# Sixth layer of a fused six-layer block: the norm of the next tile, the rounding of its x and the products of its scales move from VectorE to GpSimd

## Chip, cores and metric

One core of a Trainium2 chip runs the whole program in one launch. The metric is device time in microseconds (us); the median of 3 runs of the kernel before is 2464.33 us (2462.03 to 2466.09). DVE is VectorE, ACT is ScalarE, PE is TensorE, POOL is GpSimd, SP is SyncE.

## The reference, cut to the sixth layer

Six layers follow one another on x of 64x32 tokens by 256 channels: three attention or FFN layers with a cross attention first, then again cross attention, attention, and a mixture of experts. The change touches the last one alone:

```
x = x + _L1_ffn_ref(_layernorm(x), router_w, gate_w, up_w, down_w)

xq     = clip(round(x * s), -128, 127) / s,   s = 127 / max(max|x|, 1e-5)    # per token
combine = top-2 of softmax(x @ router_w.T), renormalised to sum 1
for e in range(8):
    gate, up  = xq @ gate_q[e].T, xq @ up_q[e].T          # 256 -> 512, ternary weights
    activated = up * square(relu(gate))
    y_e       = quant(activated) @ down_q[e].T            # 512 -> 256
    out      += combine[:, e] * y_e
```

The input of the layer is normalised per token (mean and variance over 256 channels), and the experts see it rounded to whole numbers; the scales of input and weights are multiplied back later.

## The kernel before, in words

The 2048 tokens are 16 tiles of 128 tokens, one per partition. x stays in SBUF (`x_all`) through all layers. Each layer is a phase with one hand-written instruction stream per engine; semaphores alone order the engines against one another, and every instruction that needs the result of the one before it on its own engine waits for it too (`link`).

In the sixth phase (`experts`) the weights of all 8 experts are in SBUF already, as bf16. A tile is worked as 4 pairs of experts, u = 0 to 3. For a pair, PE multiplies the rounded input with the gate and up weights of two experts into four PSUM banks (L2592), ACT takes relu and square (L2409, L2413), DVE multiplies by the up half (`products`, L2504), takes the largest magnitude of each token and computes the scales on 2 columns (`sizes`, L2520 to L2528). ACT adds the magic number that rounds (L2420), DVE subtracts it and clamps to bf16 (`clamp`, L2514), PE turns the tile (L2604), ACT copies it (L2430), PE multiplies by the down weights (L2616), and DVE adds the scaled result to x (`output`, L2538). Clamp runs one pair later and output two pairs later, so the pipeline runs on across tiles.

The next tile's input is prepared inside the current tile's steps. After pair 0 of tile t, DVE runs `rounded(t+1)`: norm to `f_xn` (L154), largest magnitude (L2460), scale and its reciprocal (L2461, L2462), x times scale plus magic number to `f_nxf` (L2463), minus magic number and clamp to bf16 `f_nx` (L2464), then square and cube of the scale and the product with the 8 weight scales to `f_kf` (L2465 to L2467). PE turns `f_xn` in pair 1 for the router and `f_nx` in pair 2 (L2568, L2579). DVE runs the router's softmax parts after pairs 2 and 3. `f_kf` is read by L2523 and L2526 of the following tile. `rounded(0)` stands before the loop. GpSimd does nothing in this phase but one memset at its start (L2379).

Of the kernel before, what the change touches and what calls it, by code (L numbers as in the profile page):

```python
# [18 lines left out]
ALU = mybir.AluOpType  # L19
# [3 lines left out]
P = 128  # L23
# [4 lines left out]
NT = B * S // P  # L28
# [5 lines left out]
MAGIC = 12582912.0  # L34
# [5 lines left out]
NE, IE = 8, 512  # L40
# [44 lines left out]
def build(nc, d, out):  # L85
# [2227 lines left out]
    def experts(sb):  # L2313
# [27 lines left out]
        xn_ready, xT_psum, xT_ready = shared("xn_ready", 1, NT), shared("xT_psum", 1, NT), shared("xT_ready", 1, NT)  # L2341
        lg_psum, lg_in, lg_exp = signal("f_lg_psum"), signal("f_lg_in"), signal("f_lg_exp")
        nx_ready, nxT_psum, nxT_ready = signal("f_nx_ready"), shared("nxT_psum", 1, NT), shared("nxT_ready", 1, NT)
        link = chain("f_link", 20)
        PAIRS = NE // 2
        up_psum, rg_done, sq_done, a_done = (signal("f_up_psum", NE), signal("f_rg_done", NE), signal("f_sq_done", NE),
                                             signal("f_a_done", NE))
# [29 lines left out]

        def pool(eng):
            eng.memset(magic[:, :], MAGIC).then_inc(magic_ready.sem, 1)  # L2379

# [62 lines left out]
        def vector(dve):  # L2445
            norm_vector(dve, n)
            dve.wait_ge(wr_loaded.sem, wr_loaded.at(1, 0))
            wlink_n = chain("f_wlink2", 3)
            w3 = f_ws[:, 0, :].rearrange("p (e k) -> p e k", k=3)
            wlink_n.link(dve, dve.tensor_tensor(ec[:, 0, :], w3[:, :, 0], w3[:, :, 0], ALU.mult))  # L2450
            wlink_n.link(dve, dve.tensor_tensor(ec[:, 0, :], ec[:, 0, :], w3[:, :, 1], ALU.mult))
            wlink_n.link(dve, dve.tensor_scalar(ec[:, 1, :], w3[:, :, 2], 1.0 / 127.0, None, ALU.mult))
            wlink_n.end()

            def rounded(t, s):
                link.at(t)
                normed(dve, xn[:, :], t).then_inc(xn_ready.sem, 1)
                dve.wait_ge(xn_ready.sem, xn_ready.at(t, 1))

                link.link(dve, dve.tensor_reduce(xs[:, 0:1], xn[:, :], AX.X, ALU.max, apply_absolute_value=True))  # L2460
                link.link(dve, dve.tensor_scalar(xs[:, 0:1], xs[:, 0:1], EPS, 1.0 / 127.0, ALU.max, ALU.mult))  # L2461
                link.link(dve, dve.reciprocal(xs[:, 1:2], xs[:, 0:1]))  # L2462
                link.link(dve, dve.tensor_scalar(nxf[:, :], xn[:, :], xs[:, 1:2], MAGIC, ALU.mult, ALU.add))  # L2463
                dve.tensor_scalar(nx[:, :], nxf[:, :], MAGIC, 127.0, ALU.subtract, ALU.min).then_inc(nx_ready.sem, 1)  # L2464
                link.link(dve, dve.tensor_tensor(xs[:, 2:3], xs[:, 0:1], xs[:, 0:1], ALU.mult))  # L2465
                link.link(dve, dve.tensor_tensor(xs[:, 3:4], xs[:, 2:3], xs[:, 0:1], ALU.mult))
                link.link(dve, dve.tensor_scalar(kf[s][:, :], ec[:, 0, :], xs[:, 3:4], None, ALU.mult))  # L2467

            def router_scores(t, s):

                dve.wait_ge(lg_psum.sem, lg_psum.at(t, 1))
                link.link(dve, dve.tensor_copy(lg[:, 0, :], ps[:, 1, 0:NE]))
                link.link(dve, dve.tensor_reduce(ls[:, 0:1], lg[:, 0, :], AX.X, ALU.max))
                dve.tensor_scalar(lg[:, 1, :], lg[:, 0, :], ls[:, 0:1], None, ALU.subtract).then_inc(lg_in.sem, 1)

            def router_shares(t, s):
                dve.wait_ge(lg_exp.sem, lg_exp.at(t, 1))
                link.link(dve, dve.reciprocal(ls[:, 2:3], ls[:, 1:2]))
                link.link(dve, dve.tensor_scalar(lg[:, 3, :], lg[:, 2, :], ls[:, 2:3], None, ALU.mult))

                pj, pi = spread(lg[:, 3, :], 1, NE), spread(lg[:, 3, :], 2, NE)
                dve.tensor_tensor(cmp_[:, 0, :, :], pj, pi, ALU.is_gt)
                link.link(dve, dve.tensor_tensor(cmp_[:, 1, :, :], pj, pi, ALU.is_equal))
                link.link(dve, dve.tensor_tensor(cmp_[:, 1, :, :], cmp_[:, 1, :, :], lower[:, :, :], ALU.mult))
                link.link(dve, dve.tensor_tensor(cmp_[:, 0, :, :], cmp_[:, 0, :, :], cmp_[:, 1, :, :], ALU.add))
                link.link(dve, dve.tensor_reduce(lg[:, 4, :], cmp_[:, 0, :, :], AX.X, ALU.add))
                link.link(dve, dve.scalar_tensor_tensor(lg[:, 5, :], lg[:, 4, :], TOP_K - 0.5, lg[:, 3, :],
                                                        ALU.is_lt, ALU.mult))
                link.link(dve, dve.tensor_reduce(ls[:, 3:4], lg[:, 5, :], AX.X, ALU.add))
                link.link(dve, dve.reciprocal(ls[:, 4:5], ls[:, 3:4]))  # L2490
                link.link(dve, dve.tensor_scalar(cmb[s][:, :], lg[:, 5, :], ls[:, 4:5], None, ALU.mult))
                link.link(dve, dve.tensor_tensor(oc[s][:, :], cmb[s][:, :], ec[:, 1, :], ALU.mult))
                link.end()

            def step(t, s, more, first=False):
                elink.at(t)

                def products(u):
                    for k in range(2):
                        e = 2 * u + k  # L2500
                        dve.wait_ge(sq_done.sem, sq_done.at(t, e + 1))
                        if k == 0 and not (first and u < 2):
                            dve.wait_ge(nh_done.sem, nh_done.at(t, u - 1))
                        dve.tensor_tensor(act_[u % 2][:, k, :], ps[:, 3 + 2 * k, :], rg2[k][:, :], ALU.mult)\  # L2504
                            .then_inc(a_done.sem, 1)

                def clamp(u):

                    if u >= PAIRS or (first and u < 0):
                        return  # L2510
                    dve.wait_ge(q_done.sem, q_done.at(t, u + 1))
                    if not (first and u < 2):
                        dve.wait_ge(hT_psum.sem, hT_psum.at(t, u - 1))
                    dve.tensor_scalar(nh[u % 2][:, :, :], act_[u % 2][:, :, :], MAGIC, 127.0, ALU.subtract, ALU.min)\  # L2514
                        .then_inc(nh_done.sem, 1)

                def sizes(u):
                    am, two = ams[u], slice(2 * u, 2 * u + 2)
                    dve.wait_ge(a_done.sem, a_done.at(t, 2 * u + 2))
                    dve.tensor_reduce(am[:, 0, :], act_[u % 2][:, :, :], AX.X, ALU.max, apply_absolute_value=True)\  # L2520
                        .then_inc(max_done.sem, 1)
                    dve.wait_ge(max_done.sem, max_done.at(t, u + 1))
                    elink.link(dve, dve.tensor_tensor(am[:, 1, :], am[:, 0, :], kf[s][:, two], ALU.mult))  # L2523
                    elink.link(dve, dve.tensor_scalar(am[:, 1, :], am[:, 1, :], EPS, None, ALU.max))
                    elink.link(dve, dve.reciprocal(am[:, 2, :], am[:, 1, :]))
                    dve.scalar_tensor_tensor(am[:, 3, :], am[:, 2, :], 127.0, kf[s][:, two], ALU.mult, ALU.mult)\  # L2526
                        .then_inc(size_done.sem, 1)
                    dve.tensor_tensor(am[:, 4, :], am[:, 1, :], oc[s][:, two], ALU.mult)  # L2528

                def output(u):  # L2530

                    if first and u < 0:
                        return
                    dve.wait_ge(y_psum.sem, y_psum.at(t, u + 1))
                    x = x_all[:, t if u >= 0 else t - 1, :]
                    for k in range(2):
                        dve.wait_ge(y_out.sem, y_out.at(t, 2 * u + k))
                        dve.scalar_tensor_tensor(x, ps[:, 7, k * HID:k * HID + HID], ams[u % PAIRS][:, 4, k:k + 1], x,  # L2538
                                                 ALU.mult, ALU.add).then_inc(y_out.sem, 1)
                    if u == -1:  # L2540
                        dve.wait_ge(y_out.sem, y_out.at(t, 0))
                        finish_tile(dve, n + 1, t - 1)

                for u in range(PAIRS if more else PAIRS + LAG):
                    if u < PAIRS:
                        products(u)
                        sizes(u)
                    clamp(u - 1)
                    output(u - LAG)
                    if u in (0, 2, 3) and more:  # L2550
                        parts[(0, 2, 3).index(u)](t + 1, 1 - s)
                elink.end()
                if not more:
                    dve.wait_ge(y_out.sem, y_out.at(t, NE))
                    finish_tile(dve, n + 1, t)

            parts = (rounded, router_scores, router_shares)
            tiles(dve, parts, step, written_out=True)

# [231 lines left out]
```

## Time and profile before

| | |
|---|---|
| median of the runs | 2464.33 us |
| the profiled execution | 2459.65 us |
| its span | 2457.8 us |
| mean granted TensorE clock | 0.908 |
| sixth layer, from the end of layer five | about 2024.8 to 2451.1 us |

The span runs from the first to the last instruction; the profiled execution's own time is 1.85 us longer, and the median of the runs is 4.68 us above it. A row of the timeline gives start, duration, engine, line, operation and tiles, and in brackets the idle time of the engine before it with what ended it. Rows of groups give count, busy time and mean of one.

### The profile page before, as it was taken

What the parts mean: (1) busy time and instruction counts of PE and PEld (TensorE: products, weight loads), DVE (VectorE), ACT (ScalarE), POOL (GpSimd) and SP (SyncE); (2) the same over time, 40 slices, a digit from 0 to 9 for tenths busy, and PEclk for the clock granted to TensorE, in tenths of its full rate; (3) what the DMA queues carried; (4) which work ended last, traced back from release to release, by engine and by line L of the source; (5) the groups of instructions that cost most, each with busy time, mean ns of one, the idle gap of its engine ahead of it and who ended that gap; (6) DMA issues with size and microseconds to landing.
All of it is one profiled execution on the core that took longest, in us unless ns stands there. A gap on an engine that the chain in (4) does not pass through costs nothing.

```text
span 2457.8 us, 49875 instructions
## 1 busy us (share of the span) xinstructions
PE 2009.3 (82%) x15486; PEld 1430.1 (58%) x15486; DVE 1862.2 (76%) x5158; ACT 1396.5 (57%) x3709; POOL 473.9 (19%) x561
## 2 busy tenths in 40 slices
PE   7999999999997786666799999999867766676665
PEld 6777777777775554333577677677555543333333
DVE  5588877777776456896678778777457778999997
ACT  1355555556563343443466666666555657777776
POOL 0011111111110000110334334333134430000000
PEclk9999999999998898676899999999968878988898
DMA  2011111111110101000011211111010000000000
GB/s 100 10 31 30 30 30 30 30 30 30 30 27 22 66 1 71 25 1 35 19 57 57 61 55 56 54 37 32 20 27 10 10 9 1 0 0 0 0 0 35
DMA packets 64750, 71.76 MB, mean 29 GB/s; under 512 B 40402, under 2 KB 42131, under 8 KB 63636
## 3 DMA queue, kind: packets, MB, share of 16 engines
q1 hardware_dynamic: 64660, 70.73, 9.9%
q8 instruction: 36, 0.59, 0.1%
q14 instruction: 54, 0.44, 0.1%
HBM read 63.47 MB, written 2.10 MB: 27 GB/s over the span
## 4 chain that ended last, share of the span: by engine, by line
PE 60%; DVE 27%; issue 6%; ACT 5%; DMA 1%; DVEq 0%; POOL 0%; SPq 0%; ACTq 0%; POOLq 0%
PE ps L648 5%; PE ps L619 5%; PE ps L610 4%; PE ps L632 4%; PE ps L680 3%; PE ps L1842 3%; DVE f_ams L2520 3%; DVE f_act L2504 3%; PE ps L1825 2%; PE ps L1782 2%; PE ps L1772 2%; PE ps L581 2%; PE ps L2205 2%; PE ps L1851 2%; DVE d_ks L1624 2%
## 5 line engine op out<-in xcount | busy, mean ns | idle before, releaser
L363 ACT ACTIVATE a_pr<-ps,a_nm 128x257 f32<-128x257 f32 x512 | 238.1, 473 | 182.8 <-DVE a_nm L478 182.8
L486 DVE COPY a_pT<-ps 128x512 f32<-128x512 f32 x256 | 170.3, 686 | 92.6 <-PE ps L648 92.1
L1574 ACT ACTIVATE d_pr<-d_st,d_nm 128x257 f32<-128x257 f32 x256 | 128.2, 502 | 193.7 <-DVE d_nm L1694 176.3
L478 DVE TENSOR_REDUCE a_nm<-ps 128x2 f32<-128x514 f32 x256 | 174.9, 683 | 0.0
L2592 PE MATMUL ps<-f_wt,f_nxT 128*128 128x512 bf16 x512 | 157.1, 462 | 18.2 <-DVE f_act L2504 17.7
L648 PE MATMUL ps<-ident,a_pr 128*128 128x128 f32 x1024 | 160.4, 279 | 0.0
L2616 PE MATMUL ps<-f_wt,f_nhT 128*128 128x256 bf16 x512 | 77.5, 302 | 83.8 <-ACT f_nhT L2430 83.8
L1825 PE MATMUL ps<-d_kc,d_qc 128*128 128x257 f32 x512 | 144.2, 406 | 0.0
L303 POOL TENSOR_TENSOR a_sf<-a_sf,a_ratio 128x256 f32<-128x256 f32 x64 | 39.4, 615 | 507.1 <-DVE a_ratio L507 507.1
L648 PEld LDWEIGHTS ps<-ident,a_pr 128*128 128x128 f32 x1024 | 117.5, 140 | 33.4 <-issue 12.7
L610 PE MATMUL ps<-a_cT,a_wqk 128*128 128x257 f32 x512 | 132.7, 381 | 2.9 <-DVE a_k L451 1.7
L619 PE MATMUL ps<-a_wvg,a_cT 128*128 128x256 f32 x512 | 127.6, 392 | 0.0
L2409 ACT ACTIVATE f_rg<-ps 128x512 f32<-128x512 f32 x128 | 75.6, 591 | 86.8 <-PE ps L2592 86.7
L1690 DVE CUSTOM_DVE_ANT_0 d_st<-ps,d_wm 128x257 f32<-128x257 f32 x256 | 98.7, 424 | 28.3 <-issue 25.6
L1488 POOL TENSOR_TENSOR d_qc<-d_qc,d_qs 128x512 f32<-128x512 f32 x64 | 94.4, 1475 | 105.3 <-DVE d_qs L1635 105.3
L1555 ACT ACTIVATE d_pr<-d_pr,d_ri 128x257 f32<-128x257 f32 x256 | 114.5, 496 | 0.0
L1483 POOL TENSOR_TENSOR d_kc<-d_kc,d_ks 128x257 f32<-128x257 f32 x64 | 60.0, 938 | 278.9 <-DVE d_ks L1624 255.4
L2592 PEld LDWEIGHTS ps<-f_wt,f_nxT 128*128 128x128 bf16 x512 | 56.6, 115 | 97.6 <-issue 40.4
L619 PEld LDWEIGHTS ps<-a_wvg,a_cT 128*128 128x128 f32 x512 | 92.0, 189 | 34.7 <-issue 24.8
L2616 PEld LDWEIGHTS ps<-f_wt,f_nhT 128*128 128x128 bf16 x512 | 48.5, 105 | 103.8 <-ACT f_nhT L2430 53.1
L1825 PEld LDWEIGHTS ps<-d_kc,d_qc 128*128 128x128 f32 x512 | 95.0, 196 | 22.7 <-issue 11.3
L1782 PE MATMUL ps<-d_qcT,d_qw 96*128 (+1 forms) x512 | 77.0, 296 | 33.5 <-DVE d_ks L1624 24.4
(350 smaller groups left out, 5328.6 us busy)
## 6 DMA issues: line engine op xcount, KB each, us to landing
a_cT<-in_ctx SPq DMA_DIRECT2D x64, 257.0 KB, 2.7
d_cT<-in_ctx SPq DMA_DIRECT2D x64, 257.0 KB, 2.8
f_wf<-in_f_w SPq DMA_DIRECT2D x24, 512.0 KB, 3.8
a_vbd<-a_vself SPq DMA_DIRECT2D x256, 8.0 KB
e_vb<-e_vs SPq DMA_DIRECT2D x256, 8.5 KB
c_wf<-in_c_w SPq DMA_DIRECT2D x3, 1024.0 KB, 8.3
x_all<-in_x SPq DMA_DIRECT2D x1, 2048.0 KB, 7.8
d_wo<-in_d_wo SPq DMA_DIRECT2D x1, 2048.0 KB
```

What stands on the lines that cost most here:

```text
L363: ins = act.activation(pr[j][:, g, :], ps[:, S_BANK[u % 2] + k, S:LK], ACT.Exp, bias=nm[j][:, g:g + 1], accum_out=ssum[j][:, 0, g:g + 1])
L478: dve.tensor_reduce(nm[j][:, 2 * u:2 * u + 2], ps[:, s0:s0 + 2, S:LK], AX.X, ALU.max, negate=True).then_inc(max_ready.sem, 1)
L486: dve.tensor_copy(pT[u][:, :, :, :], ps[:, T_BANK[u % 2], :].rearrange("p (g c q) -> p g c q", g=2, c=2))\
L610: ins = pe.matmul(ps[:, P_BANK, 0:LC], lhsT=wqk[:, 2, k, m * P:m * P + P], rhs=cT[j][:, k, :], start=(k == 0), stop=(k == KT - 1))
L619: ins = pe.matmul(ps[:, P_BANK, c * HID:c * HID + HID], lhsT=cT[j][:, k, c * P:c * P + P], rhs=wvg[:, k, :], start=(k == 0), stop=(k == KT ...
L648: ins = pe.transpose(ps[:, T_BANK[u % 2], (2 * k + c) * P:(2 * k + c + 1) * P], pr[j][:, 2 * u + k, c * P:c * P + P], ident[:, :])
L1555: ins = act.activation(pr[j][:, g, :], pr[j][:, g, :], ACT.Copy, scale=ri[j][:, g:g + 1])
L1574: ins = act.activation(pr[j][:, g, :], st[u][:, k, :], ACT.Exp, bias=nm[u][:, k:k + 1], accum_out=sm[j][:, g:g + 1])
L1782: ins = pe.matmul(ps[:, P_BANK, e * P:e * P + P], lhsT=qw[:, g * HA + e, :], rhs=qcT[:, tile_cols(tile)], start=True, stop=True)
L1825: ins = pe.matmul(ps[:, S_BANK[u] + k, 0:LC], lhsT=qc[s // BT][:, g, s % BT, :, :].rearrange("p h q -> p (h q)"), rhs=kc[j][:, :], start=T ...
L2592: ins = pe.matmul(ps[:, 2 + 2 * k + w, :], lhsT=nxT[s][:, c, :], rhs=wt[:, 3 * e + w, c * IE:c * IE + IE], start=(c == 0), stop=(c == KT - 1))
L2616: ins = pe.matmul(ps[:, 7, k * HID:k * HID + HID], lhsT=nhT[u % 2][:, k, c, :], rhs=wt[:, 3 * e + 2, c * HID:c * HID + HID], start=(c == 0 ...
```

## The change

GpSimd gets a loop over the 16 tiles. It norms tile t into `f_xn` as soon as PE has turned the one before (and, in its own order, after the rounding and the products of tile t-1), rounds and clamps `f_nxf` to `f_nx` once DVE has written it, and does the three small products of the scales. DVE keeps the reduction, the scale, its reciprocal and the product with the magic number, and waits for `f_xn` (from GpSimd now), for the last `f_nx` before it overwrites `f_nxf`, and for `f_kf` before L2523 of pair 0.

```diff
-        link = chain("f_link", 20)
+        link, plink = chain("f_link", 16), chain("f_plink", 2)
+        nxf_ready, kf_ready = signal("f_nxf_ready"), signal("f_kf_ready")
...
         def pool(eng):
             eng.memset(magic[:, :], MAGIC).then_inc(magic_ready.sem, 1)
+            eng.wait_ge(rstd_ready.sem, rstd_ready.at(n, 1))
+
+            def normed_input(t):
+                eng.wait_ge(xT_psum.sem, xT_psum.at(t, 0))
+                eng.tensor_scalar(xn[:, :], x_all[:, t, :], mv_all[:, t, 0:1], rstd_all[:, t:t + 1], ALU.subtract,
+                                  ALU.mult).then_inc(xn_ready.sem, 1)
+
+            def rounded_input(t, s):
+                eng.wait_ge(nxf_ready.sem, nxf_ready.at(t, 1))
+                eng.wait_ge(nxT_psum.sem, nxT_psum.at(t, 0))
+                eng.tensor_scalar(nx[:, :], nxf[:, :], MAGIC, 127.0, ALU.subtract, ALU.min).then_inc(nx_ready.sem, 1)
+                plink.at(t)
+                plink.link(eng, eng.tensor_tensor(xs[:, 2:3], xs[:, 0:1], xs[:, 0:1], ALU.mult))
+                plink.link(eng, eng.tensor_tensor(xs[:, 3:4], xs[:, 2:3], xs[:, 0:1], ALU.mult))
+                eng.tensor_tensor(kf[s][:, :], ec[:, 0, :], xs[:, 3:4].to_broadcast([P, NE]), ALU.mult)\
+                    .then_inc(kf_ready.sem, 1)
+                plink.end()
+
+            for t in range(NT):
+                normed_input(t)
+                rounded_input(t, t % 2)
...
             def rounded(t, s):
                 link.at(t)
-                normed(dve, xn[:, :], t).then_inc(xn_ready.sem, 1)
                 dve.wait_ge(xn_ready.sem, xn_ready.at(t, 1))
...
                 link.link(dve, dve.reciprocal(xs[:, 1:2], xs[:, 0:1]))
-                link.link(dve, dve.tensor_scalar(nxf[:, :], xn[:, :], xs[:, 1:2], MAGIC, ALU.mult, ALU.add))
-                dve.tensor_scalar(nx[:, :], nxf[:, :], MAGIC, 127.0, ALU.subtract, ALU.min).then_inc(nx_ready.sem, 1)
-                link.link(dve, dve.tensor_tensor(xs[:, 2:3], xs[:, 0:1], xs[:, 0:1], ALU.mult))
-                link.link(dve, dve.tensor_tensor(xs[:, 3:4], xs[:, 2:3], xs[:, 0:1], ALU.mult))
-                link.link(dve, dve.tensor_scalar(kf[s][:, :], ec[:, 0, :], xs[:, 3:4], None, ALU.mult))
+                dve.wait_ge(nx_ready.sem, nx_ready.at(t, 0))
+                dve.tensor_scalar(nxf[:, :], xn[:, :], xs[:, 1:2], MAGIC, ALU.mult, ALU.add).then_inc(nxf_ready.sem, 1)
...
                     dve.wait_ge(max_done.sem, max_done.at(t, u + 1))
+                    if u == 0:
+                        dve.wait_ge(kf_ready.sem, kf_ready.at(t, 1))
                     elink.link(dve, dve.tensor_tensor(am[:, 1, :], am[:, 0, :], kf[s][:, two], ALU.mult))
```

## Rows read from the trace of the kernel before

**Rows 1.** Page, busy time by engine: us, share of the span, instructions.
```profile
PE 2009.3 (82%) x15486; PEld 1430.1 (58%) x15486; DVE 1862.2 (76%) x5158; ACT 1396.5 (57%) x3709; POOL 473.9 (19%) x561
```

**Rows 2.** Busy time by stretch, sixth layer; columns PE, PEld, DVE, ACT, POOL, clock.
```profile
2036.00:2451.00 415.00, 277.33 (x1648) 148.45 (x1648) 380.06 (x1082) 310.89 (x505) 0.00 (x0) 0.87 0.00 0
```

**Rows 3.** Waits of DVE in that stretch: us in total, times, longest.
```profile
DVE f_act L2504 <- ACT f_rg L2413: 5.2, 10, 0.9
```

**Rows 4.** Timeline, DVE alone, one tile's preparation: start us, us, line.
```profile
2219.90 0.40 DVE L154 TENSOR_SCALAR f_xn<-x_all,mv_all,rstd_all 128x256 f32<-128x256 f32 x1
2220.34 0.42 DVE L2460 TENSOR_REDUCE f_xs<-f_xn 128x1 f32<-128x256 f32 x1
...
2221.18 0.35 DVE L2463 TENSOR_SCALAR f_nxf<-f_xn,f_xs 128x256 f32<-128x256 f32 x1
...
2222.42 1.29 DVE L2504 TENSOR_TENSOR f_act<-ps,f_rg 128x512 f32<-128x512 f32 x2
2223.74 1.22 DVE L2520 TENSOR_REDUCE f_ams<-f_act 128x2 f32<-128x1024 f32 x1
2225.00 0.16 DVE L2523 TENSOR_TENSOR f_ams<-f_ams,f_kf 128x2 f32<-128x2 f32 x1
...
2225.60 0.16 DVE L2526 SCALAR_TENSOR_TENSOR f_ams<-f_ams,f_kf 128x2 f32<-128x2 f32 x1
```

**Rows 5.** Groups of instructions by line, DVE in 2036 to 2451.
```profile
L154 DVE TENSOR_SCALAR f_xn<-x_all,mv_all,rstd_all 128x256 f32<-128x256 f32 x15 | 6.1, 405 | 0.0
```

**Rows 6.** Groups of POOL by form, whole span: count, busy us, mean ns.
```profile
L1498 POOL TENSOR_SCALAR d_wm<-d_dist 128x257 f32<-128x257 f32 x64 | 69.3, 1083 | 5.4
```

**Rows 7.** One line's instructions, L1076: ns min/median/max, first and last start.
```profile
L1076 POOL TENSOR_TENSOR c_hm<-c_hm,c_power x16: 189/637/638, 989.1 to 1136.4; 128x1 f32<-128x1 f32 x16
```

**Rows 8.** Timeline, DVE and POOL in the third layer.
```profile
997.38 1.23 DVE L1221 TENSOR_TENSOR c_h<-c_h,c_g 128x1024 f32<-128x1024 f32 x1
998.02 0.64 POOL L1076 TENSOR_TENSOR c_hm<-c_hm,c_power 128x1 f32<-128x1 f32 x1 [7.59 <-ACT c_junk L1109]
998.73 0.56 POOL L1077 TENSOR_TENSOR c_hm<-c_hm,c_power 128x1 f32<-128x1 f32 x1
```

**Rows 9.** Timeline, DVE and POOL in the fifth layer.
```profile
1905.43 0.72 POOL L2007 TENSOR_TENSOR x_all<-x_all,e_yb 128x256 f32 x1
1905.54 0.76 DVE L154 TENSOR_SCALAR e_xn<-x_all,mv_all,rstd_all 128x256 f32 x1 [0.39 <-DVE e_rc L2151]
...
1911.99 3.36 POOL L2004 TENSOR_TENSOR e_kn<-e_kn,e_half 128x16 f32<-128x16 f32 x1
1912.50 0.74 DVE L2140 SCALAR_TENSOR_TENSOR e_tt<-e_sc,e_gs,e_ob 128x512 f32<-128x512 f32 x1
```

**Rows 10.** One line's instructions: L154 in the fifth layer, and L1690.
```profile
L154 DVE TENSOR_SCALAR e_xn<-x_all,mv_all,rstd_all x16: 411/758/761, 1789.6 to 1987.5; 128x256 f32 x13, 128x256 f32<-128x256 f32 x3
...
L1690 DVE CUSTOM_DVE_ANT_0 d_st<-ps,d_wm x256: 420/422/429, 1196.2 to 1767.3; 128x257 f32<-128x257 f32 x128
```

**Rows 11.** Timeline: squares on ACT and the products after them, two tiles.
```profile
2124.02 0.63 ACT L2413 ACTIVATE f_rg<-f_rg 128x512 f32<-128x512 f32 x1
...
2124.45 1.27 DVE L2504 TENSOR_TENSOR f_act<-ps,f_rg 128x512 f32<-128x512 f32 x2
...
2226.02 0.63 ACT L2413 ACTIVATE f_rg<-f_rg 128x512 f32<-128x512 f32 x1
...
2227.72 1.27 DVE L2504 TENSOR_TENSOR f_act<-ps,f_rg 128x512 f32<-128x512 f32 x2
```

**Rows 12.** Timeline, start of the sixth layer.
```profile
2027.81 0.25 DVE L146 RECIPROCAL rstd_all<-std_all 128x16 f32<-128x16 f32 x1 [1.62 <-ACT std_all L151]
...
2028.71 0.41 DVE L154 TENSOR_SCALAR f_xn<-x_all,mv_all,rstd_all 128x256 f32<-128x256 f32 x1
...
2031.34 0.37 PE L2579 MATMUL ps<-ident,f_nx 128*128 128x128 bf16 x2
```

**Rows 13.** One line's instructions on POOL's queue, L297.
```profile
L297 POOLq MODIFY_POOL_CONFIG  x2: 11/11/11, 100.5 to 100.6; - x2
```

## The prediction

> **What bounds the kernel now.** I read the page first: over the whole span PE is busiest and POOL idles most of the time [rows 1]. That is a mean over six layers, so the second view is the busy time by stretch, for the sixth layer alone, from the first product to the last output [rows 2]. There DVE is busy 380.06 of 415.00 us, ACT 310.89, PE 277.33, POOL nothing. Third, what DVE waits for in that stretch: ten waits on ACT's squares, 5.2 us together [rows 3]. Nearly all the rest of its idle time is the short gap between an instruction and the next that needs its result. So DVE sets the pace of this layer, and time taken off DVE should come back nearly whole, as long as the ring PE, ACT, DVE has slack. Fourth, the timeline of DVE through one tile's preparation, for what is removed [rows 4].
>
> **What the change removes on DVE.** Before, the preparation ran from the start of L154 at 2219.90 to the start of the first product at 2222.42, 2.52 us. Two pieces of it go. The norm: from 2219.90 to the start of the reduction at 2220.34, 0.44 us. The rounding, the two squares and the product of the scales: from the end of L2463 (2221.18 + 0.35 = 2221.53) to 2222.42, 0.89 us. About 0.05 more goes since the product needs no result of the instruction before it: independent instructions stand closer than their durations (the two products take 1.29 us for 2 and L2504's neighbours start while one ends). Together 1.38 us a tile. It happens 15 times inside the steps [rows 5], once before them.
>
> **What it adds on DVE.** Two waits a tile stand newly in DVE's queue, for the last `f_nx` (done a tile ago) and for `f_kf` (written 20 us before). Both are met long before. No row shows the issue of a met wait; between 0 and 0.05 us each from the gaps of rows 4 (reduction's end 2224.96 to L2523 at 2225.00 is 0.04, with a wait in it); I take 0.05 for both, net 1.33. Were one of them late, the reduction, the products and PE's next gate and up matmuls would stand behind it.
>
> **Is `f_xn` there in time?** GpSimd starts it once it has finished the scales of the tile before, some 3 us after that tile's `f_nxf`, and DVE wants it some 23 us later: a whole tile of cover. If GpSimd needed more than that, DVE would stand at the reduction; the durations below are far from it. `f_nx` is wanted by PE in pair 2, and with a GpSimd duration of even 2 us it is there about 2 us after L2463, while PE comes to it behind the clamp that ends about 5 us after L2463 (2226.4). `f_kf` is wanted a tile later. PE's turn of `f_xn` comes earlier by its wait, which frees nothing behind it: the down matmuls after it wait for ACT.
>
> **GpSimd's own durations.** This trace has no norm with two scalars per partition on POOL. The nearest row is its tensor_scalar of two operations on 257 elements, 1083 ns [rows 6]; another op of 256 elements took 0.72 us [rows 9]. So D, the time of each of the two big ones, is bounded by 0.72 below and, for want of a row with such scalars, by 2.0 above: an estimate, the 1.08 of the row nearest to it and again as much for reading the scalars. I take 1.08. The small products: 0.19 us undisturbed [rows 7], each with 0.07 for the handover (998.02 + 0.64 to 998.73) [rows 8]; the product over 8 columns I put at 0.24, a little above the single column.
>
> **What it costs DVE: the two engines block one another.** In the third layer [rows 8] POOL's L1076 on one element starts under DVE's L1221, which reads two SBUF tensors and ends at 998.61; POOL's ends at 998.66, 0.64 us, where the undisturbed one took 0.189 [rows 7]. The other way [rows 9]: DVE's norm starts at 1905.54 under POOL's L2007 (ends 1906.15) and ends at 1906.30, 0.76 instead of 0.41 us (the same op's minimum) [rows 10]. A DVE op with one input from PSUM and one from SBUF doesn't suffer: L1690 takes 420 to 429 ns in all 256, POOL busy beside many [rows 10]. So what matters is which DVE op GpSimd's big ones meet.
>
> Count from the end of L2463, T = 0. `f_nx` on GpSimd from 0.07 to 0.07 + D; the squares to 0.59 + D; `f_kf` to 0.90 + D; the next `f_xn` from 0.97 + D to 0.97 + 2D. DVE in this time: products (PSUM and SBUF, not touched) and the reduction over one tensor, until L2523 at 2.58 (2225.00 - 2222.42). L2523 reads two SBUF tensors. With D = 1.08 `f_xn` runs from 2.05 to 3.13 and holds L2523 for 0.55 us. All is fixed in phase, so it happens in every tile: 2D - 1.61 a tile, nothing below D = 0.8.
>
> The Trainium skill, "SBUF — State Buffer", section "Who interferes with whom", says the shared port pair is locked for a whole instruction and the loser blocks fully. The first pair of rows 9 agrees; the second pair doesn't: DVE's L2140, two SBUF inputs, ran 0.74 us at 1912.50 inside a POOL op of 3.36 us, so there the lock wasn't held to the end. By the page the toll is 0.55 us a tile; if only the streaming part locks it is less, down to nothing.
>
> **PE and ACT.** Is DVE's earlier product ready to run? In pair 2 the second square ended at 2226.65 and the second product began about 2228.37 (2227.72 + 0.65): slack 1.72. The tightest of those I looked at is 2124.65 against 2125.10, 0.45 [rows 11]. With 0.78 us a tile gained, some 3 tiles in 15 wait about 0.3: I take 1 us in all.
>
> **The start of the layer.** `rounded(0)` is in the open. GpSimd can start the norm at 2028.15, just after the reciprocal (2027.81 + 0.25), while DVE came to it at 2028.71 behind three small products: with D = 1.08 it ends at 2029.23, against 2029.12. Rounding on GpSimd ends near 2031.6 (L2463 would end 0.1 later, at 2030.45), while PE turned `f_nx` at 2031.34 [rows 12]: 0.3 us lost, to the first gate matmul.
>
> **The sum.** 15 x (1.33 - 0.55) = 11.7, less 1 and 0.3, 10.4 us. The profiled execution, 2459.65 us, would come to 2449.3; the median of the runs stands 4.7 above that execution, so 2464.3 - 10.4 = 2453.9 us.
>
> **Rivals.**
> (a) No collision. D below 0.8, or the lock held only in part. For it: 0.72 for another 256-element op. Against: the tensor_scalar row at 1.08. 15 x 1.33 = 20, less 0.3 and 1 to 2.5 for tighter slack: 2446 to 2448, say 2447 us.
> (b) A deep collision, D of 1.2 to 1.47, `f_xn` ending 0.8 to 1.3 us after L2523 is due: 15 x (1.33 - 1.05) = 4, less 1: 2461 us.
> (c) Slower: GpSimd's hold on the shared reads. Where D passes 1.47 us, 2D - 1.61 exceeds 1.33 and each tile loses. At D = 2.0 `f_xn` starts at 2.97, behind L2523, and holds L2526, due at 3.18 (0.60 after L2523) [rows 4], to 4.97: 1.79 - 1.33 = 0.46 a tile, 7 us, and 1 at the start: 2472 us. For it: scalars per partition appear on POOL in no row. Against: rows 6.
> (d) The ring of PE and ACT takes over: they hold half of what DVE gives up, 2459 us. For it: ten waits on the squares exist [rows 3] and the clock stood at 0.87 of 2.4 GHz in this stretch [rows 2]. Against: ACT is busy only 311 of 415 us, and three quarters of the gain would still be inside the usual slack of 1.72.
> (e) The change doesn't do what it says for time: GpSimd's results come late somewhere I count as covered, and DVE stands at `f_xn` or PE at `f_nx` for about 1.3 us a tile, 2464 us.
> (f) A first use of code on GpSimd delays `rounded(0)`, in the open, by about 6 us: 2460 us. The one kind of configuration entry on POOL's queue took 11 ns, twice [rows 13], which speaks against it. The Trainium skill, "GPSIMD Engine Reference", section "Instruction dispatch", says the first call of freshly loaded code pays about 6 us; both operations used here ran in earlier layers, and nothing in this trace shows such a pause.
>
> **Chances.** Forecast 0.40; (a) 0.22; (b) 0.14; (c) 0.08; (d) 0.08; (e) 0.05; (f) 0.03. Under 0.2%, 4.9 us, this kernel can't be told from no change. Faster beyond it: the forecast and (a), 0.62, half of (d) 0.04, two in seven of (b) 0.04, most of (f) 0.02: 0.72. Slower beyond it: most of (c), 0.07. The same: 0.21. The range goes from 2445 (rival (a) with no loss to slack) to 2463 (the end of (b)) and leaves out (c), (e) and the edges, under 2 in 10.
>
> **What would show it.** Right: in the profile after, groups of L154's old work on POOL near 1.08 us, DVE's `f_xn` group gone, and L2523 in pair 1 alone grown from 0.16 to about 0.7 us while the same line in other pairs stays; tiles 25.0 us apart, where they were 25.8 (the starts of `f_xn` at 2039.8 and 2400.7, 14 tiles). L2523 unchanged everywhere is (a). L2526 or the clamp grown is (b) or (c), by D. More than 15 us of DVE waits on squares is (d). A gap before the first gate matmul over 3 us is (f). The prediction is wrong if DVE's removed 1.3 us a tile reappears as waits that none of these names.

## The result and the profile after

The changed kernel takes 2441.12 us (median of 4 runs, 2438.91 to 2443.30) against 2463.18 (4 runs, 2461.57 to 2466.09): ratio 0.9909, 95% interval 0.9892 to 0.9926. That is 22.1 us faster. Forecast were 10.4 us, with about 17 us (2447 us) as the rival without a collision; the time lies below the stated range.

The sign and the place were right, the size was not. From profile to profile the start of the sixth layer moves although the code ahead of it is the same (2020.88 us in one of the runs below, 2034.96 in another), so I measure the layer by itself, from the start of the reciprocal L146 to the issue of the output's store: before 2451.14 - 2027.81 = 423.3 us, after 403.6 us.

Timeline of the changed kernel, DVE's and POOL's rows of one tile (start us, us, engine, line), then the end of the layer:

```profile
2030.25 0.25 DVE L146 RECIPROCAL rstd_all<-std_all 128x16 f32<-128x16 f32 x1 [1.62 <-ACT std_all L151]
2030.62 1.25 POOL L2385 TENSOR_SCALAR f_xn<-x_all,mv_all,rstd_all 128x256 f32<-128x256 f32 x1 [3.31 <-DVE rstd_all L146]
...
2213.46 0.41 DVE L2481 TENSOR_REDUCE f_xs<-f_xn 128x1 f32<-128x256 f32 x1
...
2214.29 0.35 DVE L2485 TENSOR_SCALAR f_nxf<-f_xn,f_xs 128x256 f32<-128x256 f32 x1
2214.56 1.28 DVE L2522 TENSOR_TENSOR f_act<-ps,f_rg 128x512 f32<-128x512 f32 x2
2214.72 1.07 POOL L2391 TENSOR_SCALAR f_nx<-f_nxf 128x256 bf16<-128x256 f32 x1 [21.00 <-DVE f_nxf L2485]
2215.87 1.22 DVE L2538 TENSOR_REDUCE f_ams<-f_act 128x2 f32<-128x1024 f32 x1
2215.88 0.19 POOL L2393 TENSOR_TENSOR f_xs<-f_xs 128x1 f32<-128x1 f32 x1
...
2216.42 0.20 POOL L2395 TENSOR_TENSOR f_kf<-f_ec,f_xs 128x8 f32<-128x8 f32 x1
2216.61 1.22 POOL L2385 TENSOR_SCALAR f_xn<-x_all,mv_all,rstd_all 128x256 f32<-128x256 f32 x1
2217.13 0.16 DVE L2543 TENSOR_TENSOR f_ams<-f_ams,f_kf 128x2 f32<-128x2 f32 x1
...
2217.88 0.69 DVE L2532 TENSOR_SCALAR f_nh<-f_act 128x1024 bf16<-128x1024 f32 x1
...
2433.89 0.35 SPq L2674 DMA_DIRECT2D out<-x_all  x1
```

From the reduction to the first product are 1.10 us, where [rows 4] have 2.52 from the norm on. POOL's chain runs in the order in which the prediction counted it. And here is the surprise: the norm on GpSimd runs from 2216.61 to 2217.83, L2543 (the old L2523) starts inside it, at 2217.13, and still takes its 0.16 us. Second, the layer as a stretch (columns as in [rows 2]), and DVE's largest wait:

```profile
2036.00:2434.00 398.00, 265.90 (x1655) 147.09 (x1653) 363.15 (x1017) 312.80 (x511) 42.17 (x75) 0.88 0.00 0
```

```profile
DVE f_act L2522 <- ACT f_rg L2435: 5.0, 9, 1.1
```

DVE is still the busiest, 91%, and its waits on ACT's squares haven't grown from [rows 3]. Third, over all tiles, the line where the toll was expected and POOL's norm (ns min/median/max):

```profile
L2543 DVE TENSOR_TENSOR f_ams<-f_ams,f_kf x64: 160/161/164, 2042.2 to 2422.6; 128x2 f32<-128x2 f32 x64
...
L2385 POOL TENSOR_SCALAR f_xn<-x_all,mv_all,rstd_all x16: 1223/1224/1245, 2030.6 to 2362.4; 128x256 f32<-128x256 f32 x16
```

So the norm costs GpSimd 1.22 us and the rounding 1.07, and by the prediction's way of counting (the norm from 0.97 + 1.07 = 2.04 to 3.26 us after `f_nxf`'s end, L2523 due at 2.58) the toll would be 0.68 us a tile. None was paid. The table gives the layer and the interval between the starts of the f_xs reduction, the shortest and the mean, for all kernels:

| kernel | layer, us | shortest tile | mean tile |
|---|---|---|---|
| before | 423.3 | 25.53 | 25.78 |
| changed | 403.6 | 24.10 | 24.32 |
| norm alone on GpSimd | 420.0 | 25.24 | 25.51 |
| rounding and products alone | 409.4 | 24.53 | 24.80 |
| norm later, under the clamp | 401.6 | 24.09 | 24.33 |
| two-tensor op added | 416.5 | 25.03 | 25.35 |
| changed, again | 402.6 | 24.10 | 24.32 |
| norm 0.2 us before L2543's time | 404.5 | 24.23 | 24.45 |
| two more products | 392.7 | 23.52 | 23.74 |
| the router on GpSimd | 391.4 | 21.50 | 23.43 |

(Each row is one profile. The mean is over 14 intervals, from tile 1's reduction on; the shortest leaves out the first of them, which still belongs to the filling of the pipeline.)

### The profile page after: what moved, and what is told of

The parts are those of the page before. It is cut to its first block, busy times and chain, and to the rows that moved or that the text cites. A ratio compares the mean times of both kernels' runs of the same rounds, so it can differ in the third digit from the quotient of the medians.

```text
span 2441.5 us, 49923 instructions
## 1 busy us (share of the span) xinstructions
PE 1999.1 (82%) x15486; PEld 1429.0 (59%) x15486; DVE 1843.2 (75%) x5078; ACT 1395.8 (57%) x3709; POOL 519.7 (21%) x641
## 4 chain that ended last, share of the span: by engine, by line
PE 60%; DVE 26%; issue 7%; ACT 5%; POOL 1%; DMA 1%; DVEq 0%; SPq 0%; ACTq 0%; POOLq 0%
PE ps L648 5%; PE ps L619 5%; PE ps L610 5%; PE ps L632 4%; PE ps L680 3%; DVE f_act L2522 3%; DVE f_ams L2538 3%; PE ps L1842 3%; PE ps L1825 3%; PE ps L1772 3%; PE ps L1782 3%; PE ps L581 2%; PE ps L1851 2%; PE ps L2205 2%; PE ps L1807 2%
## 5 line engine op out<-in xcount | busy, mean ns | idle before, releaser
L2612 PE MATMUL ps<-f_wt,f_nxT 128*128 128x512 bf16 x512 | 148.0, 441 | 7.4 <-DVE f_act L2522 6.9
L1690 DVE CUSTOM_DVE_ANT_0 d_st<-ps,d_wm 128x257 f32<-128x257 f32 x256 | 98.7, 424 | 29.1 <-issue 26.5
L363 ACT ACTIVATION_READ_ACCUMULATOR a_pr<-ps,a_nm 128x1 f32 x512 | 102.8, 201 | 0.0
```

Of the source, the lines that this page charges most:

```text
L363: ins = act.activation(pr[j][:, g, :], ps[:, S_BANK[u % 2] + k, S:LK], ACT.Exp, bias=nm[j][:, g:g + 1], accum_out=ssum[j][:, 0, g:g + 1])
L2612: ins = pe.matmul(ps[:, 2 + 2 * k + w, :], lhsT=nxT[s][:, c, :], rhs=wt[:, 3 * e + w, c * IE:c * IE + IE], start=(c == 0), stop=(c == KT - 1))
```

## Experiments

Two theories for the missing toll stood at first. By size: a short VectorE op slips past GpSimd, a long one is held (made to wait). By kind: GpSimd's ops on one tensor hold nothing, only its two-tensor ops do. The prediction's own theory, a hold for the whole op, was already refuted by the row of L2543.

**The norm alone.** Rounding and products stay on DVE.

```diff
             def rounded_input(t, s):
                 eng.wait_ge(nxf_ready.sem, nxf_ready.at(t, 1))
-                eng.tensor_scalar(nx[:, :], nxf[:, :], MAGIC, 127.0, ALU.subtract, ALU.min).then_inc(nx_ready.sem, 1)
...
-                eng.tensor_tensor(kf[s][:, :], ec[:, 0, :], xs[:, 3:4].to_broadcast([P, NE]), ALU.mult)\
-                    .then_inc(kf_ready.sem, 1)
```

> Only the norm of the next tile on GpSimd; the rounding and the scale products stay on VectorE. In the changed kernel the norm's departure shortened VectorE's tile by 0.45 us (output's start to the reduction's start, 1.36 to 0.91 us), with no toll in return. If the two parts simply add, 15 x 0.45 = 6.8 us, less about 0.1 at the start: 2456.5 us where the kernel before has 2463.2. If part of the gain came from the two together (VectorE's whole preparation out of the ring's way), less than 5 us here. If GpSimd's norm holds VectorE after all, the gain is under 3 us and L2523 (0.16 us) is longer in pair 1.

Measured: 2460.31 against 2461.01 us, ratio 0.9997 (0.9978 to 1.0016): in whole times no change, where 6.8 us were expected. The layer is 3.4 us shorter, the shortest tile 0.28 us and not 0.45. Timeline, where the missing 0.17 us goes:

```profile
2199.73 0.29 DVE L2478 TENSOR_SCALAR f_nx<-f_nxf 128x256 bf16<-128x256 f32 x1
2199.80 1.32 POOL L2385 TENSOR_SCALAR f_xn<-x_all,mv_all,rstd_all 128x256 f32<-128x256 f32 x1 [24.38 <-DVE f_nxf L2476]
2199.94 0.15 DVE L2479 TENSOR_TENSOR f_xs<-f_xs 128x1 f32<-128x1 f32 x1
2200.12 0.33 DVE L2480 TENSOR_TENSOR f_xs<-f_xs 128x1 f32<-128x1 f32 x1
```

Here GpSimd starts the next norm as soon as `f_nxf` is written, while DVE still rounds. The square (L2479) at 0.14 us into it passes, the cube (L2480) at 0.32 takes 0.33 us for the 0.16 it had. So a one-column op is held: the theory by size falls, and so does the one by kind, since the GpSimd op that holds it reads one tensor.

**Rounding and products alone.** The norm stays on DVE.

```diff
-                eng.tensor_scalar(xn[:, :], x_all[:, t, :], mv_all[:, t, 0:1], rstd_all[:, t:t + 1], ALU.subtract,
-                                  ALU.mult).then_inc(xn_ready.sem, 1)
...
                 link.at(t)
+                normed(dve, xn[:, :], t).then_inc(xn_ready.sem, 1)
```

> Only the rounding of x and the three scale products on GpSimd; VectorE norms the tile itself. The changed kernel has 0.27 us from the start of f_nxf to the first product where there were 1.24: 0.97 us a tile. If the parts add: 15 x 0.97 = 14.6, less 0.5 at the start (GpSimd's rounding takes 1.07 us in the open, VectorE's 0.29): 2449 us. If slack in the ring limits it, 10 to 12 us.

Measured: 2451.36 us (2449 were expected), ratio 0.9957 (0.9936 to 0.9977); layer 13.9 us shorter, shortest tile 1.0 us shorter. By the layer the parts are 3.4 and 13.9, 17.3 together against 19.7 for both. The 0.17 us toll of the norm alone, 2.5 us over 15 tiles, is as large as the difference: with both parts gone from DVE, that op isn't there to be held.

**The norm under the clamp.** GpSimd holds its norm back until DVE's largest magnitudes of pair 1 are out.

```diff
                 eng.wait_ge(xT_psum.sem, xT_psum.at(t, 0))
+                if t >= 2:
+                    eng.wait_ge(max_done.sem, max_done.at(t - 2, 2))
```

> The changed kernel, but GpSimd holds its norm back until VectorE's largest magnitudes of pair 1 are out, so that its 1.22 us lie over VectorE's two-column scale ops and over the clamp of 1024 columns (0.687 us undisturbed). In the changed kernel the norm ends 0.05 us before the clamp starts. Theory by size (a short VectorE op slips by, a long one on the shared second port is held): the clamp starts 0.6 us into the norm and is held until it ends, about 0.6 us longer, 15 x 0.5 = 8 us slower than the changed kernel, 2449. Theory by kind (GpSimd's op on one tensor holds nothing, only its two-tensor ops do): clamp 0.687 as ever, time as the changed kernel, 2441.

Measured: 2438.79 us, ratio 0.9919 (0.9890 to 0.9949), the layer as in the changed kernel or 1 to 2 us less.

```profile
2208.05 1.53 POOL L2387 TENSOR_SCALAR f_xn<-x_all,mv_all,rstd_all 128x256 f32<-128x256 f32 x1 [0.66 <-DVE f_ams L2540]
2208.10 0.17 DVE L2546 TENSOR_SCALAR f_ams<-f_ams 128x2 f32<-128x2 f32 x1
...
2208.50 0.16 DVE L2548 SCALAR_TENSOR_TENSOR f_ams<-f_ams,f_kf 128x2 f32<-128x2 f32 x1
...
2208.65 0.69 DVE L2534 TENSOR_SCALAR f_nh<-f_act 128x1024 bf16<-128x1024 f32 x1
```

It is GpSimd that pays: the norm takes 1.53 us for 1.22, and the clamp, started 0.6 us into it, its usual 0.69. So it goes in 13 of the 14 tiles. In the other one the clamp comes later, 0.88 us into the norm, and there DVE pays:

```profile
2135.28 1.23 POOL L2387 TENSOR_SCALAR f_xn<-x_all,mv_all,rstd_all 128x256 f32<-128x256 f32 x1 [0.65 <-DVE f_ams L2540]
...
2136.16 0.89 DVE L2534 TENSOR_SCALAR f_nh<-f_act 128x1024 bf16<-128x1024 f32 x1 [0.20 <-issue]
```

So a long op isn't held as such, as the theory by size had it, but the norm has a second moment, late in it, at which it can hold one.

**A two-tensor op at the same moment.** GpSimd multiplies 512 columns of two tensors into a scratch tile, then norms.

```diff
+                if t >= 2:
+                    eng.wait_ge(max_done.sem, max_done.at(t - 2, 2))
+                    eng.tensor_tensor(junk[:, :, :], x_all[:, t - 1:t + 1, :], x_all[:, t - 1:t + 1, :], ALU.mult)
```

> The same moment, but first an added GpSimd tensor_tensor that reads two tensors of 512 columns and writes a scratch tile (1.25 us), then the norm. It lies over the four two-column ops and the clamp. Theory by size: two-column ops stay at 0.16 us, the clamp is held about 0.6 us, 2449 us. Theory by kind: the ops of two SBUF tensors (L2543, L2546) are held as well as the clamp, so L2543 grows by up to 1.2 us; 15 x 1.2 = 18 us slower than the changed kernel, 2459.

Measured: 2453.67 us, ratio 0.9964 (0.9941 to 0.9987); shortest tile 0.93 us longer than in the changed kernel, layer 12.9 us longer.

```profile
2200.15 0.16 DVE L2547 TENSOR_TENSOR f_ams<-f_ams,f_kf 128x2 f32<-128x2 f32 x1
2200.26 1.04 POOL L2388 TENSOR_TENSOR f_junk<-x_all 128x512 f32<-128x512 f32 x1 [0.61 <-DVE f_ams L2542]
2200.34 0.98 DVE L2548 TENSOR_SCALAR f_ams<-f_ams 128x2 f32<-128x2 f32 x1
2201.29 1.48 POOL L2389 TENSOR_SCALAR f_xn<-x_all,mv_all,rstd_all 128x256 f32<-128x256 f32 x1
...
2201.55 0.29 DVE L2550 SCALAR_TENSOR_TENSOR f_ams<-f_ams,f_kf 128x2 f32<-128x2 f32 x1
```

This op holds DVE almost to its end: a tensor_scalar of 2 columns takes 0.98 us for 0.17, and ends with it. The norm behind it then holds L2550, which starts 0.26 us into it, for 0.13 us. 0.81 + 0.13 = 0.94 us a tile, as good as the 0.93 that the shortest tile grew by.

**Pairs of ops by themselves.** None of the layers is computed: each GpSimd form is set beside each DVE form.

> None of the layers is computed: the kernel only sets pairs of ops side by side. GpSimd starts one op (the norm form on 256 or 1024 columns, the rounding form on 256, a two-tensor multiply on 256 or 512, a two-tensor add on 256) while VectorE runs a reduction and then one of eight forms (tensor_scalar of 1024, 256 or 2 columns, the clamp of 1024, tensor_tensor of 256 or 2, scalar_tensor_tensor of 2, a reduction of 256); each VectorE form also runs beside nothing. Theory by size: beside any GpSimd op the forms of 256 columns and more (not the reduction) are longer than alone by up to the rest of the GpSimd op, the two-column forms are not. Theory by kind: beside the norm and rounding forms everything is as alone; beside the two-tensor ops the two-port and two-tensor forms are longer, the two-column ones too. First theory (a full lock): all but the reduction are longer beside all six.

One run. Timeline (x4 is four instructions of DVE in a row; the first row, DVE's four with nothing beside them):

```profile
6.42 0.36 DVE L130 TENSOR_TENSOR tt_with_none<-src 128x2 f32<-128x2 f32 x4
...
13.44 1.76 POOL L113 TENSOR_SCALAR pool_xn<-src,scal 128x256 f32<-128x256 f32 x1 [0.23 <-DVE lead L163]
13.59 0.68 DVE L128 TENSOR_SCALAR nh_with_xn<-src 128x1024 bf16<-128x1024 f32 x1
...
17.14 1.24 POOL L113 TENSOR_SCALAR pool_xn<-src,scal 128x256 f32<-128x256 f32 x1 [0.22 <-DVE lead L163]
17.28 0.57 DVE L130 TENSOR_TENSOR tt_with_xn<-src 128x2 f32<-128x2 f32 x4
...
37.86 0.72 POOL L116 TENSOR_TENSOR pool_tt<-src 128x256 f32<-128x256 f32 x1 [0.64 <-DVE lead L163]
38.03 1.10 DVE L128 TENSOR_SCALAR nh_with_tt<-src 128x1024 bf16<-128x1024 f32 x1
...
40.96 0.78 DVE L130 TENSOR_TENSOR tt_with_tt<-src 128x2 f32<-128x2 f32 x4
...
72.03 3.80 POOL L113 TENSOR_SCALAR pool_xn<-src,scal 128x1024 f32<-128x1024 f32 x1 [0.22 <-DVE lead L163]
72.18 1.21 DVE L130 TENSOR_TENSOR tt_with_xn<-src 128x2 f32<-128x2 f32 x4
```

What DVE's four two-column ops lose, by the GpSimd op beside them: norm of 256 columns 0.57 - 0.36 = 0.21 us of that op's 1.24; norm of 1024 columns 0.85 us of 3.80; rounding of 256 0.09 of 1.07; two-tensor op of 256 0.42 of 0.72. Behind the norm of 256 columns DVE has finished its four ops 0.71 us after the norm's start, with half a microsecond of the norm to run. And an op of DVE that starts 0.15 us into the norm gets in first: the clamp keeps its 0.68 us and the norm takes 1.76. Beside the two-tensor op it doesn't: the clamp starts 0.17 us into it and takes 1.10. Reductions lose nothing beside any of them.

None of the three theories holds as a whole. What fits all rows, here and in the layer, is this. GpSimd's norm of 256 columns keeps DVE off in two short stretches of itself.
**The norm moved onto L2543.** If so, the toll was over-priced, and in the changed kernel L2543 misses even the small one by its phase, its place in time against the norm. A memset of about 0.3 us ahead of each norm shifts it.

```diff
                 eng.wait_ge(xT_psum.sem, xT_psum.at(t, 0))
+                if t >= 2:
+                    eng.memset(junk[:, 0:256], 0.0)
```

> The changed kernel, unaltered, on the same chip as the three below. From the end of the fifth layer's wait (start of the reciprocal L146) to the store of the output 403.6 us, where the kernel before has 423.3; its shortest tile 24.10 us against 25.53. If the sixth layer repeats so, what varies in the whole time from run to run (2452 to 2465 us for the kernel before) lies in the five layers ahead of it.

> The changed kernel with a GpSimd memset of a 256-column scratch tile ahead of each norm but the first two (0.31 us, it reads nothing), so that the norm starts some 0.2 us before VectorE's L2543 (160 ns) in pair 1 and not 0.5. The kernel of pairs showed that the norm on 256 columns holds a two-column VectorE op of two SBUF tensors for 0.21 us if that op starts 0.2 us into it, but not the next ones. Theory of the reading part (GpSimd holds the shared port only while it reads, its first half): L2543 or L2544 of pair 1 grows to about 0.3 to 0.4 us, the shortest tile goes from 24.10 to about 24.3, 3 us in all. Rival (short ops of this kernel are never held by the norm): 0.16 and 24.10 as in the changed kernel.

Measured on one chip: the unaltered kernel 2439.51 us (ratio to before 0.9930, 0.9913 to 0.9947; 17.6 us less than the kernel before there, 2457.07), its shortest tile the same 24.10 to 0.01 us; the shifted one 2441.53 (0.9934, 0.9917 to 0.9951), shortest tile 24.23.

```profile
2218.66 1.22 POOL L2388 TENSOR_SCALAR f_xn<-x_all,mv_all,rstd_all 128x256 f32<-128x256 f32 x1
2218.93 0.29 DVE L2546 TENSOR_TENSOR f_ams<-f_ams,f_kf 128x2 f32<-128x2 f32 x1
```

The same DVE op as L2543, now 0.27 us into the norm and not 0.52, takes 0.29 us for 0.16. The toll comes back, 0.13 us a tile, in each of the 13 tiles where the two meet so: the mechanism of the forecast is real, with a quarter of its size and only at that phase. In whole times the two kernels can't be told apart.

**More work off DVE.** The first of two steps beyond the change moves the last two router products, `f_cmb` and `f_oc`, to GpSimd.

```diff
-                link.link(dve, dve.tensor_scalar(cmb[s][:, :], lg[:, 5, :], ls[:, 4:5], None, ALU.mult))
-                link.link(dve, dve.tensor_tensor(oc[s][:, :], cmb[s][:, :], ec[:, 1, :], ALU.mult))
...
+                eng.wait_ge(sum_ready.sem, sum_ready.at(t, 1))
+                plink.link(eng, eng.tensor_tensor(cmb[s][:, :], lg[:, 5, :], ls[:, 4:5].to_broadcast([P, NE]), ALU.mult))
+                eng.tensor_tensor(oc[s][:, :], cmb[s][:, :], ec[:, 1, :], ALU.mult).then_inc(oc_ready.sem, 1)
```

> The changed kernel with the last two router products (f_cmb and f_oc, 8 columns each, 0.46 us of VectorE a tile with their gaps) on GpSimd too, which waits for VectorE's reciprocal and has its result out about 0.7 us later; VectorE needs it 3 us later. If VectorE still sets the pace: 15 x 0.46 = 7 us less than the changed kernel, 2434 us where that has 2441; shortest tile 23.65. If the ring of TensorE and ScalarE has come to bind (ScalarE busy 79% in the changed kernel), under 3 us.

Measured: 2430.89 us, ratio 0.9887 (0.9871 to 0.9904), against 2439.51 for the changed kernel on that chip; layer 9.9 us shorter than the changed kernel's there, shortest tile 0.58 us (expected were 7 us and 0.45). DVE still sets the pace. In one tile the norm's second stretch meets L2551, which has 0.17 us in the others:

```profile
2311.08 1.22 POOL L2386 TENSOR_SCALAR f_xn<-x_all,mv_all,rstd_all 128x256 f32<-128x256 f32 x1
...
2311.96 0.37 DVE L2551 TENSOR_SCALAR f_ams<-f_ams 128x2 f32<-128x2 f32 x1
```

The second moves all of the router behind the exponential (14 GpSimd ops for twelve of DVE's, the softmax's division left out as it cancels).

```diff
-            parts = (rounded, router_scores, router_shares)
+            parts = (rounded, router_scores)
...
+                plink.link(eng, eng.tensor_tensor(cmp_[:, 0, :, :], pj, pi, ALU.subtract))
+                plink.link(eng, eng.tensor_tensor(cmp_[:, 0, :, :], cmp_[:, 0, :, :], lower[:, :, :], ALU.add))
+                plink.link(eng, eng.tensor_scalar(cmp_[:, 1, :, :], cmp_[:, 0, :, :], 0.0, 1.0, ALU.is_gt, ALU.mult))
...
```

> All of the router behind the exponential on GpSimd, with its sums as halving adds; the division by the softmax's sum is left out since the top two are divided by their own sum, and a tie is broken by adding 1e-30 times the order. VectorE loses 2.7 us a tile (ten ops), GpSimd gets 15 ops, about 5 us. If VectorE sets the pace: 15 x 2.7 = 40 us. But ScalarE alone is busy 20.4 us a tile, so the tile can't go below about 22: 15 to 30 us less than the changed kernel. If GpSimd's result is late for the scales of pair 0 (needed about 6 us after the exponential), VectorE waits there and the gain is under 10. If GpSimd's many two-tensor ops hold VectorE's clamp and scale ops (0.2 us each), 3 to 5 us of it go again.

Measured: 2427.95 us, ratio 0.9876 (0.9859 to 0.9892): 11.6 us less than the changed kernel, where 15 to 30 were expected, and only 2.9 less than the step before, although the shortest tile fell by another 2.0 us. Waits of DVE, and the stretch:

```profile
DVE f_act L2528 <- ACT f_rg L2457: 32.1, 45, 3.6
```

```profile
2036.00:2420.00 384.00, 262.35 (x1653) 151.50 (x1651) 330.83 (x824) 310.74 (x508) 108.48 (x298) 0.88 0.00 0
```

A tile can now be 21.5 us, but most aren't: DVE waits 32.1 us for the squares where it waited 5.0. Here the ring of PE and ACT has become the bound, rival (d) of the prediction, one change later. Neither of the two is busy all the time (262.35 and 310.74 of 384.00 us), so it is the way around that is too long; which part of it, no run here separates. GpSimd's new two-tensor ops cost DVE little: its scalar_tensor_tensor of the scales grew by 0.08 us a tile, where 3 to 5 us in all had been thought possible.

## Why the prediction was wrong, point by point

- **What bounds the layer**: right. DVE's removed time came back: 1.43 us of the shortest tile and 1.46 of the mean one, 19.7 of the layer (20.7 in the repeat).
- **What is removed, 1.38 us a tile**: about right. By the timelines 0.45 (output to reduction, 1.36 to 0.91) and 0.97 (f_nxf's start to the product, 1.24 to 0.27), 1.42.
- **The added waits, 0.05**: nothing is seen of them; the lower end of their bounds, nothing, fits.
- **GpSimd's durations, D = 1.08**: right for the rounding (1.07), a little low for the norm (1.22). The products took 0.19, 0.19 and 0.20.
- **The toll of 0.55 us a tile, 8 us in all**: this is the step that failed. The prediction let GpSimd's norm hold L2523 until the norm's end; the runs show that it holds DVE only in two short stretches of itself, and L2543, as the line is called now, kept its 0.16 us in all 64 of its instructions. The row it rested on, the norm of the fifth layer held by POOL's op [rows 9], is of a two-tensor add, which does hold almost to its end; I carried it over to a tensor_scalar. With the norm of 256 columns it is at most about 0.2 us, and in the changed kernel L2543 starts 0.52 us into it, behind the first stretch, and pays nothing. That the other ops of the scales and the clamp miss the second stretch too is luck of the phase: nothing in the prediction counted on it. The second pair of [rows 9] spoke for a partial hold and was given the smaller chance. The Trainium skill, "SBUF — State Buffer", section "Who interferes with whom", locks the pair for the whole instruction. The two-tensor op of 1.04 us about agrees (0.98 for 0.17), the norm doesn't (0.21 lost of 1.24).
- **The start, 0.3 us**: mis-sized. From L146 to the first product 8.66 us became 9.28: 0.6. The norm ended 0.3 us later against L146 than DVE's did, not 0.1 (1.25 us, not 1.08), and the rounding took 1.07 us where DVE's took 0.29; the first gate matmul, 0.6 us later against L146 than before, took over both.
- **The ring, 1 us**: not seen. DVE's waits on the squares went from 5.2 to 5.0 us, and the 14 intervals gave back 14 x 1.46 = 20.4 us, no less than 14 times the shortest tile's gain. What the layer's 19.7 lacks against 15 x 1.43 = 21.5 lies at the two ends, outside these intervals: at the start, and behind the last reduction, where the changed kernel took 50.6 us in one profile and 49.5 in the other, the kernel before 50.0.
- **The sum again**: 10.4 + 8.2 for the toll + 1.5 for 1.43 instead of 1.33 us a tile + 1 for the ring - 0.3 for the start = 20.8 us. The layer shows 19.7 and 20.7.
- **The rivals**: (a) is what happened, by a lock held only in part, priced at 2447 us with 1 to 2.5 us of waiting that wasn't seen. D below 0.8, its other way, did not happen. It had a chance of 0.22 against the forecast's 0.40, though one of the two pairs in [rows 9] spoke for it. Of the medians' 22.1 us, the last 1.4 to 2.4 aren't in this layer and are within what the medians of the kernel before wander (2463.2, 2461.0 and 2457.1 in three sets of runs). So that the time fell below the range, and not only outside the forecast, is in part this wandering.

## What to carry to other kernels

Work moved to an idle GpSimd came back almost whole here, where VectorE is busy nine tenths of the stage, until the ring behind it bound; it did once VectorE had lost another 2.0 us a tile. Price the collision of the two engines by kind of op. In these runs a GpSimd tensor_tensor multiply or add of 256 or 512 columns held VectorE's ops on SBUF tensors, reductions excepted, almost to its end. A norm-like tensor_scalar held them for a short part near its start, and a tensor_scalar of VectorE also for one near its end, and the phase decided whether even that was paid. Where a few microseconds matter, compare the stage's own length and the shortest loop interval, since the stages ahead wander by more.

## What the runs showed of the hardware that I had not expected

An op of VectorE that starts 0.15 us into GpSimd's norm goes first, and the norm takes 1.76 us for 1.24. The same GpSimd form on 1024 columns takes 3.80 us, of which VectorE's two-column ops lose 0.85. The norm can hold VectorE a second time: a tensor_scalar that starts 0.88 us into it lost 0.2 us, a clamp that starts 0.60 us into it lost nothing and made the norm 0.31 us longer. And the start of the sixth layer moved by 14 us between profiles (2020.88 to 2034.96) with nothing changed ahead of it; what causes that was not looked into.
